# Attention and a two-expert feed-forward on one core: normalisation shared out between VectorE, ScalarE and GpSimd, and one product moved in the tail

## The reference

```
x = x + gamma * attention(layernorm(x), ctx, ctx)     # 8 heads; the 128 rows are 8 heads x 16 channels, 256 positions
x = x + ffn(layernorm(x))
layernorm(x) = (x - mean) / sqrt(var + 1e-5)          # over the 256 columns
attention: softmax over 256 keys of (q^T k) / 4, times v
ffn: gate g = argmax(softmax(x Wg^T)) picks one of two experts for each row
     expert 0: gelu(x W0a^T + b0a) W0b^T + b0b ;  expert 1: relu(x W1a^T + b1a) W1b^T + b1b    # 512 hidden units each
```

## Time and profile before

| | |
|---|---|
| median of 3 runs | 233.05 us (232.84 to 233.07) |
| the profiled execution | 232.91 us in all, 231.1 us of it the span |
| PE busy | 217.1 us, 94% |
| DVE busy | 174.3 us, 75% |
| ACT busy | 145.6 us, 63% |
| POOL busy | 137.8 us, 60% |
| granted TensorE clock | full in all 40 slices |

### The profile page before, as it was taken

One profiled execution on the slowest core, in us unless ns is written; L12 is line 12 of the kernel. 1 busy time (PEld: TensorE's weight loads), 2 busy tenths in 40 slices (PEclk: granted clock), 3 DMA queues, 4 the chain that ended last, 5 costly groups with the idle time before them and its releaser, 6 DMA issues.

```text
span 231.1 us, 5325 instructions
## 1 busy us (share of the span) xinstructions
PE 217.1 (94%) x2036; PEld 165.9 (72%) x2041; DVE 174.3 (75%) x357; ACT 145.6 (63%) x220; POOL 137.8 (60%) x180
## 2 busy tenths in 40 slices
PE   7789879788999999999999999999999999899995
PEld 3334445456787978788787978797879787778995
DVE  7499977999579976997699869994888444545583
ACT  6205766856985597658784779477944986624240
POOL 6852314879889718972698358934762287382800
PEclk9999999999999999999999999999999999999999
DMA  4785499543224340625052704250302000000101
GB/s 136 244 301 185 140 372 375 176 142 139 92 85 150 113 143 16 240 67 191 4 198 74 237 1 119 94 180 33 72 1 72 0 27 3 23 26 0 47 3 45
DMA packets 19393, 26.40 MB, mean 114 GB/s; under 512 B 1992, under 2 KB 12840, under 8 KB 19112
## 3 DMA queue, kind: packets, MB, share of 16 engines
q1 hardware_dynamic: 18942, 25.66, 33.4%
q10 hardware_dynamic: 426, 0.40, 0.5%
HBM read 11.01 MB, written 2.10 MB: 57 GB/s over the span
## 4 chain that ended last, share of the span: by engine, by line
PE 76%; DVE 8%; ACT 5%; DMA 4%; issue 3%; SPq 3%; POOL 1%
PE ff L775 20%; PE ff L795 12%; PE od L722 11%; PE st L710 10%; PE ff L807 7%; PE smax L697 5%; DVE nmax L396 3%; PE od L730 3%; DMA qkst<-mlow 2%; PE od L737 2%; PE tr L748 2%; ACT P L576 2%; PE tr L758 2%; DMA qkst<-parts 1%; PE od L679 1%
## 5 line engine op out<-in xcount | busy, mean ns | idle before, releaser
L576 ACT ACTIVATE P<-st 128x1024 f32<-128x1024 f32 x64 | 66.1, 1033 | 47.7 <-PE st L710 47.3
L396 DVE TENSOR_REDUCE nmax<-smax 128x4 f32<-128x1024 f32 x56 | 68.5, 1224 | 21.3 <-PE smax L697 20.5
L267 POOL TENSOR_TENSOR mv<-mv,power 128x1 f32<-128x1 f32 x32 | 19.1, 596 | 47.9 <-DVE mv L378 47.8
L775 PE MATMUL ff<-xnTh,w1h 128*128 128x256 f32 x128 | 38.1, 298 | 1.0 <-DVE y L495 1.0
L775 PE MATMUL ff<-xnTl,w1h 128*128 128x256 f32 x128 | 36.0, 281 | 0.0
L775 PE MATMUL ff<-xnTh,w1l 128*128 128x256 f32 x128 | 35.9, 281 | 0.0
L285 POOL TENSOR_TENSOR hidL<-hid,hidH 128x1024 fp32r<-128x1024 f32 x13 | 31.0, 2386 | 6.0 <-DVE hidH L457 4.6
L609 ACT ACTIVATE hid<-ff,b1t 128x256 f32<-128x256 f32 x64 | 26.1, 479 | 12.2 <-PE ff L775 12.1
L710 PE MATMUL st<-qkst 64*128 64x256 f32 x256 | 32.2, 330 | 1.4 <-ACT P L576 0.5
L795 PE MATMUL ff<-w2h,hidH 128*128 128x256 f32 x124 | 32.1, 292 | 0.0
L722 PE MATMUL od<-P,vt 128*32 128x256 f32 x512 | 30.9, 382 | 0.0
(11 more groups left out here) (81 smaller groups left out, 369.6 us busy)
## 6 DMA issues: line engine op xcount, KB each, us to landing
qkst<-parts SPq DMA_DIRECT2D x47, 256.0 KB
xv<-in_xv SPq DMA_DIRECT2D x16, 256.0 KB, 3.0
qk<-in_qk SPq DMA_DIRECT2D x15, 256.0 KB, 3.1
out<-y SPq DMA_DIRECT2D x16, 128.0 KB, 2.7
w1t<-in_w SPq DMA_DIRECT2D x1, 1024.0 KB, 7.2
w2t<-in_w SPq DMA_DIRECT2D x1, 1024.0 KB, 7.9
qkst<-parts ACTq DMA_DIRECT2D x1, 256.0 KB
qkst<-mlow SPq DMA_DIRECT2D x16, 8.0 KB
```

The lines of the kernel that those rows point to most:

```text
L267: pool.tensor_tensor(mv[:, b % 2, 11:12], mv[:, b % 2, 10:11], power[:, 0:1], ALU.pow).then_inc(s_rstd, 1)
L396: dve.tensor_reduce(nmax[:, c % 2, :, :, j].rearrange("p a e -> p e a"), (ff if c in WIDE and j % 2 else smax)[:, :, :, :], AX.X, ALU.max, ...
L576: act.activation(P[:, b % 2, j, :, :, :].rearrange("p e a l -> p (e a l)"), st[:, :, :, :].rearrange("p e a l -> p (e a l)"), ACT.Exp, sca ...
L775: mm = pe.matmul(ff[:, u // 2 % 2, u % 2, :], w[:, a, e, m * 128:(m + 1) * 128], xs[:, i % 2, a, :], start=a == 0 and n == 0, stop=a == LC ...
```

## The change

Four edits:

- The addition of epsilon goes from DVE to POOL, for both normalisations and all batches.
- For q of batches 3 to 7 ScalarE computes `scale * q + offset` (function Identity) in place of DVE's `(q - mean) * rstd`; scale is rstd, and POOL computes the offset, -mean * rstd, in two operations. ScalarE does it just ahead of `high` of the same batch.
- The same for x1 of batches 0 and 1; their `gate` stays on DVE but comes one slot later, behind that slot's `take_max`.
- At the end, `x_norm(15)` on DVE stands ahead of `low_relu`, and `values(15)` on TensorE stands between units 1 and 2 of `gemm1(6, ...)` in place of behind unit 3.

DVE waits before statistics that overwrite what ScalarE reads (`s_qn`, `s_xn`), and where the normalisation goes back from ScalarE to DVE, DVE waits for ScalarE's last one.

```diff
+ACT_Q = range(3, 8)
+ACT_X = range(0, 2)
...
         def _(pool):
-            def rstd(b, mv, count, s_var, s_rstd):
-                pool.wait_ge(s_var, count)
+            def rstd(b, mv, s_var, s_eps, s_rstd):
+                pool.wait_ge(s_var, b + 1)
+                pool.tensor_scalar(mv[:, b % 2, 10:11], mv[:, b % 2, 9:10], EPS, None, ALU.add).then_inc(s_eps, 1)
+                pool.wait_ge(s_eps, b + 1)
                 pool.tensor_tensor(mv[:, b % 2, 11:12], mv[:, b % 2, 10:11], power[:, 0:1], ALU.pow).then_inc(s_rstd, 1)
+
+            def offset(m, count, s_neg, s_off):
+
+                pool.tensor_scalar(m[:, 12:13], m[:, 8:9], -1.0, None, ALU.mult).then_inc(s_neg, 1)
+                pool.wait_ge(s_neg, count)
+                pool.tensor_tensor(m[:, 13:14], m[:, 12:13], m[:, 11:12], ALU.mult).then_inc(s_off, 1)
+
+            def rstd1(c):
+                rstd(c, mv1, s_var1, s_eps1, s_rstd1)
+                if c in ACT_Q:
+                    pool.wait_ge(s_rstd1, c + 1)
+                    offset(mv1[:, c % 2, :], c - ACT_Q.start + 1, s_neg1, s_off1)
+
+            def rstd2(b):
+                rstd(b, mv2, s_var2, s_eps2, s_rstd2)
+                if b in ACT_X:
+                    pool.wait_ge(s_rstd2, b + 1)
+                    offset(mv2[:, b % 2, :], b - ACT_X.start + 1, s_neg2, s_off2)
...
         def _(dve):
...
-                dve.bn_aggr(m[:, 8:10], m[:, 0:6]).then_inc(s_aggr, 1)
-                dve.wait_ge(s_aggr, count)
-                dve.tensor_scalar_add(m[:, 10:11], m[:, 9:10], EPS).then_inc(s_var, 1)
+                dve.bn_aggr(m[:, 8:10], m[:, 0:6]).then_inc(s_var, 1)
...
                 for p in prepared(n - 1):
-                    q_norm(p)
+                    if p not in ACT_Q:
+                        q_norm(p)
...
-                if j == 1 and b >= 2:
+                if j == 1 and b >= 2 and b - 2 not in ACT_X:
                     x_norm(b - 2)
+                    gate(b - 2)
+                if j == 2 and b - 2 in ACT_X:
                     gate(b - 2)
...
             moments2(B - 1)
+            x_norm(B - 1)
             low_relu(LAST - 1)
-            x_norm(B - 1)
             gate(B - 1)
...
+            def act_norm(out, src, m, s_done):
+                act.activation(out, src, ACT.Identity, bias=m[:, 13:14], scale=m[:, 11:12]).then_inc(s_done, 1)
+
+            def q_norm(c):
+                act.wait_ge(s_off1, c - ACT_Q.start + 1)
+                if c == ACT_Q.start:
+                    act.wait_ge(s_qn, c)
+                act_norm(qk[:, place(c, QK), 0, :], qk[:, place(c, QK), 0, :], mv1[:, c % 2, :], s_qn)
+
+            def x_norm(b):
+                act.wait_ge(s_off2, b - ACT_X.start + 1)
+                act_norm(xn[:, b % 2, :], x1[:, b % X1, :], mv2[:, b % 2, :], s_xn)
...
                 for p in prepared(n - 2 if n > 0 else n - 1) if n else ():
+                    if p in ACT_Q:
+                        q_norm(p)
                     high(p)
                 if k == 0 and 2 <= c <= B:
                     copy_max(c - 1)
+                if j == 1 and b - 2 in ACT_X:
+                    x_norm(b - 2)
...
             transpose_att(B - 2)
-            for u in range(0, 4):
+            for u in range(0, 2):
                 gemm1(B // 2 - 2, u)
             values(B - 1)
+            for u in range(2, 4):
+                gemm1(B // 2 - 2, u)
             transpose_x(B - 2, B)
```

More of the change, by code:

```diff
@@ L132, in build @@
         s_fill = [sem(f"s_fill{n}") for n in range(4)]
-        s_stat1, s_aggr1, s_var1, s_rstd1, s_qn = map(sem, ("s_stat1", "s_aggr1", "s_var1", "s_rstd1", "s_qn"))
+        s_stat1, s_var1, s_eps1, s_rstd1, s_qn = map(sem, ("s_stat1", "s_var1", "s_eps1", "s_rstd1", "s_qn"))
         s_hi, s_lo, s_q0, s_k0hi, s_k0lo = map(sem, ("s_hi", "s_lo", "s_q0", "s_k0hi", "s_k0lo"))
@@ L138, in build @@
             sem, ("s_ods", "s_odT", "s_rden", "s_attT", "s_aT", "s_x1"))
-        s_stat2, s_aggr2, s_var2, s_rstd2, s_xn = map(sem, ("s_stat2", "s_aggr2", "s_var2", "s_rstd2", "s_xn"))
+        s_stat2, s_var2, s_eps2, s_rstd2, s_xn = map(sem, ("s_stat2", "s_var2", "s_eps2", "s_rstd2", "s_xn"))
+        s_neg1, s_off1, s_neg2, s_off2 = map(sem, ("s_neg1", "s_off1", "s_neg2", "s_off2"))
         s_lead, s_mask, s_chosen, s_xb = map(sem, ("s_lead", "s_mask", "s_chosen", "s_xb"))
@@ L311, in _ @@
             pool.wait_ge(s_const, 1)
-            rstd(0, mv1, 1, s_var1, s_rstd1)
-            rstd(1, mv1, 2, s_var1, s_rstd1)
+            rstd1(0)
+            rstd1(1)
             pool.wait_ge(s_k0hi, 1)
@@ L318, in _ @@
             low(1)
-            rstd(2, mv1, 3, s_var1, s_rstd1)
+            rstd1(2)
             pool.memset(identf[:, :], 0.0).then_inc(s_const, 1)
@@ L332, in _ @@
                 for c in prepared(n):
-                    rstd(c, mv1, c + 1, s_var1, s_rstd1)
+                    rstd1(c)
                 if j == 0 and b >= 5 and b % 2:
@@ L346, in _ @@
                 if j == 0 and b >= 2:
-                    rstd(b - 2, mv2, b - 1, s_var2, s_rstd2)
+                    rstd2(b - 2)
                 if j == 2 and b >= 2:
@@ L360, in _ @@
                     pool.tensor_tensor(w2l[:, units, :], w2t[:, units, :], w2h[:, units, :], ALU.subtract).then_inc(s_w2l, 1)
-            rstd(B - 2, mv2, B - 1, s_var2, s_rstd2)
+            rstd2(B - 2)
             masks(B - 2)
@@ L364, in _ @@
             low_hidden(LAST - 1, 0)
-            rstd(B - 1, mv2, B, s_var2, s_rstd2)
+            rstd2(B - 1)
             masks(B - 1)
@@ L371, in _, with moments @@
         def _(dve):
-            def moments(b, src, mv, count, s_stat, s_aggr, s_var):
+            def moments(b, src, mv, count, s_stat, s_var):
                 m = mv[:, b % 2, :]
@@ L384, in moments1 @@
                     dve.wait_ge(s_qk[place(c, QK)], 16 * turn(c, QK))
-                moments(c, qk[:, place(c, QK), 0, :], mv1, c + 1, s_stat1, s_aggr1, s_var1)
+                if c - 2 in ACT_Q:
+                    dve.wait_ge(s_qn, c - 1)
+                moments(c, qk[:, place(c, QK), 0, :], mv1, c + 1, s_stat1, s_var1)
             def q_norm(c):
@@ L389, in q_norm @@
                 dve.wait_ge(s_rstd1, c + 1)
+                if c == ACT_Q.stop:
+                    dve.wait_ge(s_qn, c)
                 dve.tensor_scalar(q, q, m[:, 8:9], m[:, 11:12], ALU.subtract, ALU.mult).then_inc(s_qn, 1)
@@ L427, in moments2 @@
                 dve.wait_ge(s_x1, b + 1)
-                moments(b, x1[:, b % X1, :], mv2, b + 1, s_stat2, s_aggr2, s_var2)
+                if b - 2 in ACT_X:
+                    dve.wait_ge(s_xn, b - 1)
+                moments(b, x1[:, b % X1, :], mv2, b + 1, s_stat2, s_var2)
             def x_norm(b):
@@ L434, in x_norm @@
                     dve.wait_ge(s_xT, b - 1)
+                if b == ACT_X.stop:
+                    dve.wait_ge(s_xn, b)
                 dve.tensor_scalar(xn[:, b % 2, :], x1[:, b % X1, :], m[:, 8:9], m[:, 11:12],
```

## The result

The changed kernel takes 234.14 us (median of 7 runs, 233.71 to 234.92) against 233.04 us (7 runs on the same chip, 232.65 to 233.36). The ratio is 1.0053, interval [1.0035, 1.0071]: slower by 1.1 us by the medians, 1.2 by the ratio, and above the forecast range. The profiled execution took 234.58 us, its span 232.8 us (before 231.1). The seven runs differ in the granted clock: 233.71 and 233.98 us at 1.000, 234.14 and 233.79 at 0.999 and 0.998, and 234.58, 234.92 and 234.55 at 0.992. The profile is one of the last three.

The account below looks back on a forecast made before the run. DVE and ScalarE in turn were taken to bound the kernel before 56 us, then TensorE, with two waits after 200. Start +0.60 and tail -0.95 give -0.35 us against 232.91; forecast 232.6 us, range 231.6 to 233.8.

Parts of the forecast that it names:

- the start's +0.60: Before TensorE's full stretch: POOL's low part of the hidden layer 0.8 us later, less 0.15 to 0.2 slack: +0.6 us.
- Tail: After 200 us: values fill TensorE's wait for y, and x_norm goes ahead of low_relu; together -0.95 us.
- The rival in which only the first part comes: The tail gains only from the moved values, as low_relu is late for its pass: 233.2 us; chance 0.10.
- Epsilon: At the start, moving the add to POOL lengthens the chain from variance to rstd: +0.15 us, bounds 0 and +0.34.
- The rival with a product as dear as the power: POOL becomes the bound before the first low part, its one-column product costing 0.60 us: 234.1 us; chance 0.18.
- The pass on ScalarE: ScalarE's normalisation of q, priced from the copy of k: +0.44 us each, bounds 0.40 and 0.52.
- nothing hides it: In ScalarE's full stretch the passes for batches 5 and 6 delay in full: +0.44 and +0.42 us.
- POOL's queue: From about 50.0 us POOL has 2.4 us more work, so the low part begins at 67.8, delaying TensorE: +0.6 us.
- Relief of DVE: Before 56 us DVE's 1.27 us less work counts in full: 231.6 to 232.1 us, faster; chance 0.30.
- The table load: ScalarE's normalisations each need one table load and one back, 1.28 us each: 5 us slower, 238; chance 0.02.
- the signs named: In the profile after: last wide reduce near 54.1, first product near 56.8, low pass near 70.2 behind a wait for POOL.

Follow-up runs that it names:

- e1: The kernel before with the two tail edits alone: 232.03 us, ratio 0.9952.
- e2: The changed kernel with its two tail edits undone: 234.46 us, ratio 1.0072 to the kernel before.
- e3: The changed kernel with all normalisations back on DVE, keeping epsilon on POOL and the tail edits: 232.07 us, ratio 0.9962.
- e7: The changed kernel with only q of batches 5 and 6 normalised on ScalarE, all other normalisations back on DVE: 232.96 us, ratio 1.0011.
- e5: The changed kernel with the spins of slots 12 and 14 writing a free bank, without waiting for the low part of x: 233.17 us, ratio 1.0008.
- e8: The changed kernel with the spin edit of e5 and the add_bias(1) move of e6: 235.00 us, ratio 1.0076.
- e10: The kernel before with the two tail edits and the spin edit of e5: 231.70 us, ratio 0.9938.
- e11: The changed kernel with the spin edit of e5 and add_bias(1) moved to slot 22: 232.75 us, ratio 0.9986.
- e12: As e11, but all q and epsilon back on DVE, so only the sums of batches 0 and 1 are on ScalarE: 231.76 us, ratio 0.9942.
- e4: The changed kernel with q of batches 5 and 6 back on DVE: 233.13 us, ratio 1.0002.
- e9: e4 with add_bias(1) moved to slot 22, behind both low parts of the hidden layer: 232.02 us, ratio 0.9946.
- e6: e4 with add_bias(1) moved from slot 18 to 19, behind the first low part of the hidden layer: 234.11 us, ratio 1.0053.

## Why the prediction was wrong

The sum was +0.60 - 0.95 = -0.35. Measured it is, by the ratios of the changed kernel and e1, +2.3 - 1.1 = +1.2. What failed is the start's +0.60. It was read at POOL: the low part of the hidden layer was to begin at 67.8 and began at 69.80 in the changed kernel, at 68.82 in e2 with the clock up. Three steps failed in it: the price of ScalarE's pass (0.44 us taken, 0.63 measured), POOL's wide operations, for whose meeting with DVE nothing was added (0.5 to 1.0 us), and TensorE's clock, which the prediction does not name (about 1 us in the profiled run). They are taken in turn below.

**Tail: right in its mechanism.** Forecast -0.95, measured -1.07 on the chain and -1.1 by e1, less by e2 (0.4 by the ratios, 0.85 in the traces). No wait for y was left, and x_norm ahead of low_relu did not make low_relu's pass late. The rival in which only the first part comes (0.10) is refuted.

**Epsilon: right.** +0.15 forecast, some 0.2 by e3 and e1, which is within their noise. POOL's four operations for x1 of batch 1 in the changed kernel's timeline give the prices:

```profile
51.22 0.22 POOL L271 TENSOR_SCALAR mv<-mv 128x1 f32<-128x1 f32 x1 [1.46 <-DVE mv L400]
51.52 0.57 POOL L273 TENSOR_TENSOR mv<-mv,power 128x1 f32<-128x1 f32 x1
52.17 0.24 POOL L277 TENSOR_SCALAR mv<-mv 128x1 f32<-128x1 f32 x1
52.49 0.19 POOL L279 TENSOR_TENSOR mv<-mv 128x1 f32<-128x1 f32 x1
```

Epsilon 0.22, power 0.57, negation 0.24, product 0.19 (one of the seven took 0.44, the mean is 0.23), with 0.07 to 0.08 between them. I had 0.22, 0.60, 0.22, 0.25 and 0.08. The rival with a product as dear as the power did not come true by its mechanism, and that its time, 234.1, is the measured one is luck. Its own sum has slips: 50.0 + 15.4 + 3.8 is 69.2 and not 69.6, and the start's loss passes the tail's gain from 2.7 us of extra work on, not 3.3.

**The pass on ScalarE: the term that was mis-sized.** I took 0.44 us with the wait for its end, bounds 0.40 and 0.52, from the copy in the earlier trace rows. It took 0.60 to 0.61 and 0.02 to 0.03 to the next, 0.63 in all. The copy of q of batch 5 was 0.92 us late instead of 0.4 to 0.6: one pass, and 0.29 because the weights w1, for which ScalarE waits ahead of it, came at 32.81 where they came at 32.52 (32.91 in e3, which has no pass there). Of the 0.92 some 0.26 was taken up by ScalarE's idle time ahead of the exp at 41.72 (41.06 before), so that "nothing hides it" was not quite so for batch 5. The second pass came on top of the rest: the copy of batch 6 was 1.30 late instead of 0.9 to 1.0, in e2 1.57. The row I took it from was the wrong one, because it has no operand per partition. The kernel has an operation of the same size with one such operand, the hidden activation with the bias `b1t`, 479 ns before and 478 after. Groups by line of ScalarE in the changed kernel:

```profile
L655 ACT ACTIVATE hid<-ff,b1t 128x256 f32<-128x256 f32 x64 | 26.1, 478 | 12.9 <-PE ff L825 12.9
...
L606 ACT ACTIVATE qk<-qk,mv 128x256 f32<-128x256 f32 x5 | 3.0, 598 | 1.2 <-POOL mv L279 1.2
```

None 399 ns, one 478, two 598: each adds 80 to 120. The Trainium skill ("ScalarE: Activation LUTs", section "What ACT_TABLE_LOAD costs") says that an ACTIVATE with immediate scale and bias takes 186 ns + 0.833 ns per element and each [128,1] pointer operand adds about 93 ns. For 256 elements that is 399 and, with two, an estimate of 585. The rows agree with it, and I had not weighed it. No run here changed the operands alone.

**The wait and the clock: not in the prediction.** I followed the delay only along the chain to the residual and did not ask what TensorE does meanwhile. It has nothing to do: the spins that should fill such a gap stand themselves behind the wait for the low part of x. In the changed kernel's profile it idled 1.27 us and then got the 1.2 GHz level for 3 us. The spins lost 0.63 us by this, the products behind them more: from the spins to the residual it took 0.84 us longer than in e2's profile, and the low pass came 0.98 later than there (72.24 against 71.26).

The fall does not come each time. By the mean clock of each run (0.992 or 0.993; where it fell, only the one profile shows) it came in 8 of 25 runs of the three kernels with ScalarE's passes and the wait (3 of 7 of the changed kernel, 2 of 6 of e2, 3 of 12 of e7), in 1 of 42 of the five kernels whose spins don't wait (e5, e8, e10, e11, e12), and in 3 of 70 of the kernel before, whose spins wait 0.87 us. In the runs it costs about 0.8 us in the changed kernel, 1.3 in e2, 1.7 in e7. But the wait alone does not decide it: e3 waits as long as the changed kernel and kept full clock in 6 of 6 runs, at 0.9962.

```profile
46.90 0.81 PE L731 MATMUL tr<-hid,onesb 128*128 128x512 bf16 x3 [1.27 <-DVE xnTl L481]
```

The median of the seven, 234.14, is itself a run at 0.999. The four runs of the changed kernel without the fall have a mean of 233.9, and e5's median is 233.17: 0.6 to 0.7 us, by the kernel before of either set of runs, would then be the wait itself. The traces don't show so much of it: e5's first product is 0.20 and its low pass 0.28 us ahead of e2's, and in the kernel before the removal of the wait brought 0.3 at most (e10). The rest stays open.

**POOL's queue: right mechanism, other size.** As forecast, POOL takes the place of the first product: the changed kernel's chain of waits runs over POOL from the power at 51.52 to the low part at 69.84. I counted +0.6. The low pass started at 69.59 before and was 1.67 us later in e2, which has both delays at full clock; with the passes alone it was 0.81 later (e7, 70.40), with POOL's part alone 1.08 (e4, 70.67). Both delays lie one behind the other on POOL, which begins behind the residual, and so they add for the most part. POOL was to begin at 50.0 and need 17.8 us to the low part. In e2 it began at 50.64 and needed 18.18, in the changed kernel 51.22 and 18.58. In e4 TensorE's wait for it is 0.92 us, and e9 takes it away for -1.3. What I missed is how long POOL's wide operations take. The two adds of x1 (L306 before, L330 in the others) took 1.58 us before; in e4 2.62, from POOL's timeline of before, then POOL's and DVE's of e4:

```profile
64.53 1.58 POOL L306 TENSOR_TENSOR x<-x,chosen 128x256 f32<-128x256 f32 x2
```

```profile
65.66 2.62 POOL L330 TENSOR_TENSOR x<-x,chosen 128x256 f32<-128x256 f32 x2
68.25 2.37 POOL L309 TENSOR_TENSOR hidL<-hid,hidH 128x1024 fp32r<-128x1024 f32 x1
```

```profile
65.88 0.39 DVE L416 TENSOR_SCALAR qk<-qk,mv 128x256 f32<-128x256 f32 x1
66.20 0.68 DVE L487 CAST hidH<-hid 128x1024 fp32r<-128x1024 f32 x1
```

They have slipped beside DVE's normalisation and cast, which they stood ahead of, and are 1.04 us longer: more than the whole wait of 0.92, and as long as the two DVE operations together (0.39 + 0.68). In the changed kernel the second is hit, by the cast: 0.61 us longer than the first, where the cast takes 0.68. Its chain of waits:

```profile
67.65 0.75 POOL x L330
68.47 1.36 POOL x L330
69.84 2.36 POOL hidL L309
72.24 0.75 PE ff L857 x4
```

In e9, where these two adds come at another time, they take 1.56, and 1.53 to 1.62 in every trace in which they miss that cast; in e2 and e5, where they meet it, 2.07:

```profile
77.12 1.56 POOL L330 TENSOR_TENSOR x<-x,chosen 128x256 f32<-128x256 f32 x2
```

The Trainium skill ("GPSIMD Engine Reference", section "1. Specifications") says that POOL's SBUF interfaces are shared with VectorE, with contention for DVE instructions in a 2-port mode or with two SBUF inputs. I set this aside, because the new operations are one column wide. The rows fit the rule as far as they go: which mode DVE's cast ran in, no row shows, and the section gives no price. The new operations did not have to be wide, since they pushed wide ones onto DVE's. That step failed. No run parts the two effects, though: e9 takes the adds out of POOL's queue and away from the cast at once. That the slowed adds and not the longer queue make the wait is an inference: with adds of 1.58 us e4's low part would have begun 1.04 earlier, at 67.21, 0.19 behind its time before.

**Relief of DVE: the rival is refuted.** e12 has the sums off DVE (0.41 + 0.51 of the rival's 1.27 us) with nothing else in the way, and its first product is at 56.13 where e10's is at 55.97; the ratios are 0.9942 and 0.9938. The remaining 0.35, the two adds, are off DVE in e3 and bring nothing either (0.9962 against 0.9952). **The table load** did not come either: the changed kernel has the same 14 loads as the one before, none of them in a group of the passes.

Of the signs named, the first product came at 58.48 (56.8 forecast), the last wide reduce at 55.95 (54.1), the low pass at 72.24 (70.2): 1.7 to 2.0 us late each. The residual accounts for 1.1 of that: the forecast had it 1.0 behind 47.83, and it came at 49.97. Of the low pass's 2.0 about 1.0 is the clock (e2's came at 71.26); of the other 1.1, 0.56 is e2's residual (49.39) and 0.5 the slowed adds.

## What to carry to other kernels

Moving work from a busy engine to one that is idle on average pays only if the second is idle in that stretch; ScalarE, busy 63% of the span, was full for 6 us, and TensorE's queue stood behind it. Price a moved operation by its operands as well as its shape: the row without operands per partition said 0.40 us, the pass with two of them took 0.60. And for each delay that you pass on look at what the engines do that wait for it: an idle TensorE may come back at half its clock, and a late wide POOL operation may land beside one of DVE's and take longer by it. When an operation is moved to relieve a queue, check everything that is now behind it, as e6 did not.

## What was not expected of the hardware

- The clock's fall is not the same in each execution: in the changed kernel, whose profile shows a wait of 1.27 us, it came in 3 of 7 runs; in e7, whose profile shows a wait of 1.90 us and spins at full clock, in 3 of 12. e3, whose profile shows 1.27 us too, kept full clock in all six. What decides it, no run here tells.

```profile
47.95 0.81 PE L731 MATMUL tr<-hid,onesb 128*128 128x512 bf16 x3 [1.90 <-DVE xnTl L481]
```

- Beside a wide POOL operation it can also be DVE that loses. In e4 its normalisation of q took 0.39 us at 65.88, where POOL's add was slowed; in the same execution another took 1.35 beside POOL's low part of w1 (42.53, 1.27 us). Which of the two loses, no run here tells.

```profile
42.60 1.35 DVE L416 TENSOR_SCALAR qk<-qk,mv 128x256 f32<-128x256 f32 x1
```
